# Projections moved between the iterations of an attention, unread matmuls added, and masks and scores of the last attention interleaved

## What is computed

```python
x = x + tanh(g_xattn[0]) * _L0_xattn_ref(_layernorm(x), ctx, ...)   # L0: 16 heads of 8
x = x + tanh(g_ffn[0])   * _L0_ffn_ref(_layernorm(x), w1, w2)       # F0: ternary weights, 8-bit activations, gelu
x = x + tanh(g_xattn[1]) * _L1_xattn_ref(_layernorm(x), ctx, mask)  # L1: one head of 128
x = x + tanh(g_ffn[1])   * _L1_ffn_ref(_layernorm(x), ...)          # F1: as F0, gated
x = x + tanh(g_xattn[2]) * _L2_xattn_ref(_layernorm(x), ctx, ...)   # L2: 16 heads of queries, one of keys and values
x = x + tanh(g_ffn[2])   * _L2_ffn_ref(_layernorm(x), ...)          # F2: 8 experts, each token to one
x = x + tanh(g_xattn[3]) * _L3_xattn_ref(_layernorm(x), ctx, mask)  # L3: 16 heads, key mask and causal mask
x = x + tanh(g_ffn[3])   * _L3_ffn_ref(_layernorm(x), ...)          # F3: two products and butterfly stages
```

```python
scores = q @ k.T / sqrt(8)            # L3: -1e9 where the key is masked or lies ahead
out = softmax(scores) @ v             # then one 128 x 128 product over all heads
```

## Time and profile before

| | us |
|---|---|
| three runs | 1139.74, 1144.85, 1146.22 |
| median | 1144.85 |
| the profiled execution | 1140.49 |
| its span, first to last instruction | 1138.8 |
| PE busy | 971.3 (85%) |
| DVE busy | 743.7 (65%) |
| ACT busy | 635.7 (56%) |
| POOL busy | 418.0 (37%) |

### The profile page before, as it was taken

One profiled execution on the slowest core, in us unless ns is written; L12 is line 12 of the kernel. 1 busy time (PEld: TensorE's weight loads), 2 busy tenths in 40 slices (PEclk: granted clock), 3 DMA queues, 4 the chain that ended last, 5 costly groups with the idle time before them and its releaser, 6 DMA issues.

```text
span 1138.8 us, 32253 instructions
## 1 busy us (share of the span) xinstructions
PE 971.3 (85%) x11365; PEld 732.8 (64%) x11365; DVE 743.7 (65%) x2022; ACT 635.7 (56%) x1483; POOL 418.0 (37%) x743
## 2 busy tenths in 40 slices
PE   3899999995767765679999999888889999999999
PEld 3656666663435433346777676878757777777798
DVE  3556775655997799848876654255537877774344
ACT  3556565654775566537755444545545655543366
POOL 5410244551125424211243424668530176662100
PEclk9999998995577767689987856999889988885799
DMA  6978678436789998032232201857664434430011
GB/s 175 153 87 96 59 79 86 66 48 117 179 98 160 159 161 107 0 122 78 93 114 73 78 9 46 242 158 209 194 213 160 129 132 150 150 132 2 6 35 35
DMA packets 325174, 125.01 MB, mean 110 GB/s; under 512 B 220649, under 2 KB 295433, under 8 KB 325034
## 3 DMA queue, kind: packets, MB, share of 16 engines
q1 hardware_dynamic: 318682, 106.97, 48.0%
q0 software_dynamic: 5488, 15.88, 4.6%
q10 hardware_dynamic: 864, 0.27, 0.2%
HBM read 75.86 MB, written 48.09 MB: 109 GB/s over the span
## 4 chain that ended last, share of the span: by engine, by line
PE 57%; DVE 20%; issue 8%; ACT 6%; DMA 3%; POOL 3%; SPq 1%; another core or an unknown queue 0%; ACTq 0%; DVEq 0%; POOLq 0%
PE bank L1438 7%; PE bank L1419 5%; PE bank L1382 5%; DVE nmax L1872 5%; ACT probs_space L1042 4%; PE bank L1528 3%; PE bank L1398 3%; PE bank L1777 2%; PE bank L1769 2%; PE bank L1723 2%; PE bank L1735 2%; PE bank L1537 2%; PE bank L1379 2%; DVE small L2041 2%; DVE stats L1806 2%
## 5 line engine op out<-in xcount | busy, mean ns | idle before, releaser
L1872 DVE TENSOR_REDUCE nmax<-bank 128x8 f32<-128x1024 f32 x192 | 234.2, 1220 | 155.7 <-PE bank L1398 94.4
L1042 ACT ACTIVATE probs_space<-bank 128x1024 f32<-128x1024 f32 x192 | 196.7, 1025 | 187.9 <-PE bank L1419 182.8
L1419 PE MATMUL bank<-nmax_rows,max_row 8*128 8x128 f32 x1536 | 154.0, 321 | 0.0
L1419 PEld LDWEIGHTS bank<-nmax_rows,max_row 8*128 8x128 f32 x1536 | 128.8, 211 | 22.4 <-issue 18.1
L1438 PE MATMUL bank<-probs_space,vals 128*32 128x128 f32 x3072 | 141.7, 309 | 0.7 <-issue 0.7
L1398 PE MATMUL bank<-k_rows,q_rows 32*128 32x128 f32 x1024 | 96.5, 311 | 7.0 <-DMA q_rows<-q_halves 4.9
L737 POOL TENSOR_TENSOR var_b<-stats 128x8 f32<-128x8 f32 (+3 forms) x33 | 7.3, 223 | 250.7 <-DVE stats L1806 197.7
L1438 PEld LDWEIGHTS bank<-probs_space,vals 128*32 128x32 f32 x3072 | 81.2, 119 | 20.1 <-issue 4.2
L1398 PEld LDWEIGHTS bank<-k_rows,q_rows 32*128 32x128 f32 x1024 | 80.1, 216 | 11.8 <-issue 6.0
L1382 PE MATMUL bank<-q_one,k_all 32*128 32x512 f32 x256 | 75.7, 664 | 13.8 <-ACT probs_space L1042 13.4
L1402 PE MATMUL bank<-k_one,q_all 32*128 32x512 f32 x256 | 75.7, 663 | 1.7 <-DVE nmax L1872 0.9
(11 more groups left out here) (295 smaller groups left out, 2464.2 us busy)
## 6 DMA issues: line engine op xcount, KB each, us to landing
expert_rows<-zeros SPq DMA_DIRECT2D x8, 2322.0 KB, 39.3
q_rows<-q_halves SPq DMA_DIRECT2D x64, 256.0 KB
context<-expert_w SPq DMA_DIRECT2D x31, 322.0 KB
q_halves<-q_all SPq DMA_DIRECT2D x16, 512.0 KB
k_rows<-k_halves SPq DMA_DIRECT2D x32, 256.0 KB
k_one<-expert_w SPq DMA_DIRECT2D x15, 322.0 KB
late<-_L_ffn_down_weights_dram POOLq DMA_DIRECT2D x9, 512.0 KB, 5.5
late<-in_L_ffn_up_weights_dram POOLq DMA_DIRECT2D x9, 512.0 KB, 4.6
```

The costliest lines, as they stand in the source:

```text
L1042: act.activation(probs[:, 2 * g:2 * g + 2, :, :].rearrange("k g i q -> k (g i q)"), bank_pair[1][:, :, :].rearrange("k g f -> k (g f)"), A ...
L1419: m = pe.matmul(bank[2 + s][:, i * P:(i + 1) * P], max_row[rows, i:i + 1].broadcast_to([NPART * HG, P]), nmax_rows[rows, u % 2, :], start= ...
L1872: dve.tensor_reduce(nmax[:, u % 2, :].rearrange("q (g i) -> q g i", i=HG)[:, 2 * g:2 * g + 2, :], bank_pair[0][:, :, :].rearrange("q g (i ...
```

## The change

In L2 and L3:

- The work for a quad is spread: xt where t + 8 = 4c, q where t + 7 = 4c, k where t + 6 = 4c, v where t + 5 = 4c. xn is written into `o_back` instead of `xn_quad`. q's halves and rows go first, k's behind; each engine's list follows (ACT, DVE, SP). `X_LEAD` is 12, the prologue of L2 lies at other pairs of F1, and with it the eight unread matmuls (now at t = -3), and that of L3 at other slots of F2.
- From t = NT - 2 QT = 24 on every iteration issues three unread matmuls into bank 5, also the routing iterations in F2.
- SP waits for the quad before to have landed ahead of q's DMAs.

In L3, `both_masked_scores` waits for the operands, for `t_ex` and for `t_mx` first, and then alternates the masks of both kinds and the scores of both kinds, matmul by matmul. POOL's norms for F3 stand at v = 5, 6 and 10.

In L0, the maxima are split in three bf16 parts (`NPART` = 3) on POOL (`split_maxima`, ahead of its other work for the tile), transposed as bf16, multiplied by DVE with `max_row` into `nmax_one` (128 x 512 bf16) between the two maxima of an iteration, and added by two bf16 matmuls of 512 columns a half. DVE's split and ACT's copy fall away there. `scores_of_first` waits for all of both kinds first and alternates them.

In F1 the transposed hidden layer has one bank instead of two.

```diff
-NPART = 2
+NPART = 3
+NHALF = 2
-        X_LEAD = 10
+        X_LEAD = 12
...
-        TENSOR_BETWEEN = {11: range(-X_LEAD, -6), 12: (-6,), 13: (-5,), 14: (-4, -3)}
+        TENSOR_BETWEEN = {8: range(-X_LEAD, -7), 10: (-7,), 12: (-6,), 14: (-5,)}
...
-        LAST_HEAD = {NS - 9: range(-X_LEAD, -6), NS - 8: (-6,), NS - 6: (-5,), NS - 5: (-4,), NS - 4: (-3,)}
+        LAST_HEAD = {NS - 9: range(-X_LEAD, -8), NS - 8: (-8,), NS - 7: (-7,), NS - 6: (-6,), NS - 4: (-5,), NS - 3: (-4,)}
...
+            def split_maxima(v):
+                done = 4 * v
+                whole, left = (nmax[:, v % 2, i, :].rearrange("q (g i) -> q g i", i=HG) for i in range(2))
+                rows = nmax_parts[:, v % 2, :].rearrange("q (g n i) -> q g n i", g=NG, i=HG)
+                pool.wait_ge(S("t_mx"), 2 * (v + 1))
+                past(pool, "t_mt", v - 1)
+                pool.tensor_copy(rows[:, :, 0, :], whole).then_inc(S("t_na"), 1)
+                pool.wait_ge(S("t_na"), done + 1)
+                pool.tensor_tensor(left, whole, rows[:, :, 0, :], ALU.subtract).then_inc(S("t_na"), 1)
...
+                def both_masked_scores(u, g, v, f):
+                    name, landed = operands_in(layer, v // QT)
+                    pe.wait_ge(S(name), landed)
+                    past(pe, "t_ex", 2 * (tiles + u) + g)
+                    past(pe, "t_mx", 2 * (tiles + v) + (1 - f))
+                    for b in range(HG):
+                        at = slice(HR * b, HR * b + HR)
+                        for s in range(2):
+                            rows = slice(HR * (2 * g + s), HR * (2 * g + s) + HR)
+                            pe.matmul(bank[2 + s].rearrange("k (i q) -> k i q", i=HG)[:, :, at],
+                                      future_rep[rows, b, :], over_blocks(keep_rep(rows, u, b), HG),
+                                      start=b == 0, stop=False)
+                            rows = slice(HR * (2 * f + s), HR * (2 * f + s) + HR)
+                            pe.matmul(bank[s].rearrange("q (i k) -> q i k", i=HG)[:, :, at],
+                                      past_rep[rows, b, :], over_blocks(ident_blocks_bf[rows, :], HG),
+                                      start=b == 0, stop=False)
...
-                    c = quad(t, 6)
+                    c = quad(t, 8 if own else 6)
                     if c is not None:
                         if own:
                             pe.wait_ge(S("t_xn"), own_tiles + QT * (c + 1))
-                            pe.wait_ge(S("t_kn"), quads + c + 1)
+                            past(pe, "t_ve", own_quads + c)
...
-                    c = quad(t, 6)
+                    c = quad(t, 7)
                     if own and c is not None:
                         pe.wait_ge(S("t_xe"), own_quads + c + 1)
                         pe.matmul(quad_bank(c), wq, xnT_quad[:, :], start=True, stop=True).then_inc(S("t_qp"), 1)
-                    c = quad(t, 7)
+                    c = quad(t, 6)
                     if own and c is not None:
-                        past(pe, "t_ve", own_quads + c)
+                        pe.wait_ge(S("t_qa"), quads + c + 1)
                         pe.matmul(quad_bank(c), wk, contextT[:, QT * P * c:QT * P * (c + 1)],
                                   start=True, stop=True).then_inc(S("t_kp"), 1)
-                    c = quad(t, 4)
+                    c = quad(t, 5)
...
-                        if layer == "L2" and c == 0:
-                            fill_wait(8, 3)
+                    if own and t >= NT - 2 * QT:
+                        pe.wait_ge(S("t_ve"), own_quads + NQ)
+                        fill_wait(3, 5)
```

230 lines of the change are left out of this document (142 added, 88 removed).

## The result

| | before | after |
|---|---|---|
| median, us | 1142.3 (4 runs, 1134.57 to 1146.22) | 1158.16 (4 runs, 1154.09 to 1164.28) |
| profiled execution, its span | 1140.49, 1138.8 | 1154.09, 1152.4 |
| PE, DVE, ACT, POOL busy | 971.3, 743.7, 635.7, 418.0 | 961.3, 765.7, 627.2, 446.1 |
| mean granted clock | 0.853 | 0.858 |

A forecast was written before the change was run, and what follows sets the result against it. The prediction took TensorE (PE) to bound the kernel, losing its granted clock late in L2 and L3. Its terms summed to -58.6 from the profiled 1140.5, giving 1081.9, and 1084 us with half the profile-to-median gap; range 1056 to 1115.

The forecast's parts named there:

- L3, the term of -8: L3 ahead of its tail: -5 from a steadier clock, -3 from alternating masks and scores of both kinds.
- at nothing: Parts priced at zero: F1's single bank, F3's moved norms, the memset on POOL behind L0, the wait for ACT's v copy.
- The tails, -36.1 in all: Ends of L2 (-12.8, -6.4) and L3 (-9.5, -7.4): three unread matmuls an iteration hold PE's clock.
- One tail falls: Rival: three matmuls at 1.2 GHz may not bring the clock back, one layer's tail is lost; 1115 us, chance 0.09.
- L2's middle, -6: L2, v = 18 to 25: spread projections win half the gap from lost clock; -6, ends 0 and -11.
- L2's start, -7: Start of L2: q goes a quad earlier, ending PE's wait for q_rows and relieving F1's last pairs; -7, ends -2 and -11.
- F2's +3: F2: seven routing iterations with three unread matmuls each, 4.6 us, of which two thirds show; +3, ends 0 and +4.5.
- L3's start, +1.5: Start of L3: k's copy by way of DRAM stands behind q's, costing part of a trip; +1.5, ends -2.7 and +5.
- L0, -5: L0: subtraction in two matmuls instead of eight shortens PE's halves, POOL's split hidden; -5, upper end +8.
- Transposes hold nothing: Rival: transposes hold no clock, so it still falls once in four iterations in both middles; 1095 to 1115 us, chance 0.17.
- Unread matmuls hold no clock at all: Slower rival: both tails stay at 0.50 and the matmuls only cost time; 1161 us, chance 0.04.
- what would make it wrong: Signs: a later exponential in L3, a POOL chain over 2.4 us, or a tail at 0.50 beside its unread matmuls.

The follow-up runs named there:

- before_waits_ahead: The kernel before with the wait for the maxima moved ahead of L3's masks and scores by key, order unchanged: 1166.37 us in two executions, beside 1140.46 for before.
- A: Theory that DVE's later split loses the port to POOL; put into the kernel before as one more always-met wait ahead of each split: ratio 1.0443.
- B: Theory that L3's common wait for the maxima leaves PE idle; put into the kernel before by moving that wait ahead: 1166.37 us, two executions.
- both repairs: The changed kernel with DVE's wait for zero_set once, at L2's first split, and L3's masks and scores in the old order with the old waits: 1112.6 us, 0.9956.
- the repaired kernel: The changed kernel with DVE's zero_set wait once and L3's scores in the old order and waits; run again: 1109.65 us, ratio 1.0041; without unread matmuls 1141.38, 1.008.
- repaired_xt_pool: The repaired kernel plus three unread matmuls at the iteration with only xt, and POOL in L3 waiting for the split's end: 1109.12 us, ratio 0.987.
- _no_f2: repaired_xt_pool without the 21 unread matmuls in F2's seven routing iterations: 1102.41 us, ratio 0.9897.
- after_wait_once: The changed kernel with DVE's wait for zero_set once, at L2's first split, instead of ahead of every split: 1125.04 us, ratio 1.0196.
- after_once_separate: The changed kernel with DVE's zero_set wait once and L3's masks and scores in the old order with the old waits: 1112.6 us, ratio 0.9956.
- before_met_wait: The kernel before with one more, long-met wait on DVE ahead of each split of the maxima in L2 and L3: 1150.67 us, ratio 1.0443.
- before_unread: The kernel before with only the unread matmuls of the tails and F2 added: 1142.57 us, ratio 1.0136.
- after_again: The changed kernel once more, unchanged, on the chip of the runs beside it: 1149.39 us, ratio 1.0281.

## Why the prediction was wrong

**L3, the term of -8, is the step that failed.** Ahead of the tail (v = 0 to 25) it was +27.0; with the tail, +33.3 where -17.5 was forecast, so L3 holds 50.8 of the 72.2 us between the forecast (-58.6) and the profiled execution (+13.6). Two things were wrong in it.

First, "both waits now stand ahead of everything" was seen, and priced with ends of +5 and -6. The wait costs 0.30 us an iteration (before_waits_ahead), so 30 x 0.30 = 9 us at a full clock, beyond the end of +5, and the alternation saves nothing of "the most to be saved": 1.23 us a half, before and after. And the price was taken at a fixed clock. The text asked "what stands ahead of a fall?", set idle time aside because PE was busy 19.5 of 20.5 us there, and then never asked what a longer iteration does to the clock. Put into the kernel before, A costs by the table 31.9 us by the clock beside 9.2 of work, and B 20.1 beside 3.4, B by two executions only.

Second, the list "at nothing" named the memset on POOL behind L0's last subtraction and priced the operation, not its wait. The wait stands at the head of 64 splits on DVE. It is always met, and still DVE's op starts 0.06 us later, which decides who gets the port. That row of before, 0.17 us beside a butterfly step that starts 0.04 later, and 1.33 for the op behind it, was there to be read, and no rows of the prediction hold it.

**The tails, -36.1 in all.** The mechanism held where the clock was still there: at L3's tail, 34.7 us at 1.00 with both repairs, where 41.6 - 9.5 = 32.1 was forecast. It failed in L2 of after: the fall came ahead of the first unread matmul. "One tail falls" had this case, with "the three matmuls may be too few to bring the clock back", and took the tail as lost for good; it came back after 31 us, so part was won. The price of the fills was about right: 0.66 us at 18 places of the tails and 3 us for the seven of F2, 15 in all, against 17. What was mis-sized is what the clock gives back: 36.1 + 18 x 0.66 = 48 us in the sum, 18.7 in the mean of executions of the repaired kernel. The forecast of 31.2 us for L2's v = 25 to 31 is met where the clock did hold (31.4 at 1.00, repaired_xt_pool and _no_f2). The sum rests on one trace of before with a mean clock of 0.853; executions of that kernel reach 0.892, and no trace shows what their tails look like.

**L2's middle, -6.** It was -9.3 from v = 18 to 25 but +8.6 from v = 2 to 18, where the clock fell for 14 us at v = 15, so -0.7 in all: the falls moved. In after_wait_once the early part takes 83.7 us at 1.00 against 82.0.

**L2's start, -7, came out at about -3.** The stage ahead of the first maximum gave -0.8, and v = 0 to 2 another -2.2: 9.0 us at 1.00 in all 13 traces with the new start, 11.0 to 13.4 at 0.50 to 0.74 in the seven without. PE no longer waits for `q_rows`, as said. But from the last product of F1 to the first scores it is 9.06 us before and 8.57 after, since other work has filled the gap. Before and after:

```profile
486.17 0.62 PE L1610 MATMUL bank<-ffn_wT,q_one 128*128 128x128 bf16 x8 [1.11 <-ACT q_one L1171]
486.63 1.11 PE L1565 MATMUL bank<-l_wkv,contextT 128*128 128x128 f32 x8
487.57 1.89 PE L1282 MATMUL bank<-ones_bf 128*128 128x512 bf16 x8
...
495.23 0.93 PE L1398 MATMUL bank<-k_rows,q_rows 32*128 32x128 f32 x8 [4.91 <-DMA q_rows<-q_halves]
```

```profile
478.14 1.01 PE L1685 MATMUL bank<-ffn_wT,q_one 128*128 128x128 bf16 x8 [3.40 <-DVE x L2111]
478.95 2.02 PE L1639 MATMUL bank<-l_wkv,contextT 128*128 128x128 f32 x8
...
482.63 3.30 PE L1313 MATMUL bank<-ones_bf 128*128 128x512 bf16 x8
...
486.71 0.66 PE L1418 MATMUL bank<-k_rows,q_rows 32*128 32x128 f32 x8
```

The v product takes 2.02 instead of 1.11 us and the eight unread matmuls 3.30 instead of 1.89; xt (1.09) has come in, and PE waits 0.78 for ACT ahead of it. These 4.2 us fill the wait of 4.9. The stage from v = 31 of L2 to L3's first maximum holds the last -6.4 of L2's tail, F2's +3 and L3's start, +1.5: together -1.9, and it was -2.9.

**L0, -5: right in size.** It was -6.5, and in every kernel with this L0 the stage takes 175 to 183 us, against 186 to 189 in those without. Which part of the change in L0 does it was not tried.

**The rivals.** "Transposes hold nothing" gave 1095 to 1115, with the page named there. It can't be told apart here: falls begin in iterations with only xt (912.7 in after_once_separate), but also between products (895.6 and 943.4). "Unread matmuls hold no clock at all", 1161, is near the time and false in its mechanism: taking them out of after made the ratio worse, 1.043 against 1.0281 with them (the intervals just overlap, at 1.0347 to 1.0438), and so do the granted clocks of L2's tail, 0.59 to 1.00 with them and 0.52 to 0.59 without. Its condition, 0.50 in t = 24, was met in L2 and the clock returned all the same. The sentence on what would make it wrong named "an exponential in L3 that starts later because of the maxima's wait", which happened, and "a tail at 0.50 beside its unread matmuls", which did in both layers (641.8 to 659.6 and 1028.4 to 1048.7).

## To carry to other kernels

Price a wait also where it is always met: in front of a short op of DVE that competes with POOL it can decide who starts first, so ask once, at the first use, and not in every iteration. Where the granted clock falls and returns inside a layer, as here, a step of 0.3 us in the iteration should be priced with the falls that may come with it, and an edit that raises the clock with unread matmuls must be charged for their own time at full clock; compare kernels by time and mean clock together. Before two operations of different waits are merged, look at what each did while the other's wait was open.

## What the runs showed of the hardware

- A third wait, always met, on a DVE instruction moved its start from 34 to 92 ns behind the event that it really waits for (medians of 32 tiles of L3, before and before_met_wait). With POOL's op 79 to 92 ns behind the same event, the short op took 1.53 us instead of 0.17.
- The longest stretch at a granted clock of 0.50 that began in L2's tail took 48 to 75 us in the eight traces without unread matmuls there, and 3 to 41 us in the ten of twelve with them that show one. Where it fell ahead of the first of them, it was back 18 us behind that in after, 19 in before_unread, and 1 in after_again.
- One and the same kernel before took from 1091.0 to 1180.6 us in its executions, with mean granted clocks from 0.89 down to 0.809. Medians of groups lay between 1110.1 and 1142.9.
